# Copies of turned probabilities on two engines, another rule for PSUM banks, and two projections moved, in a two-layer decoder on Trainium2

## The reference, cut to what matters

```python
x = x + _L0_attn_ref(_layernorm(x, axis=-1), ...)       # the change is here
x = x + _L0_xattn_ref(_layernorm(x, axis=-1), ...)      # and at the start of this
...
# _L0_attn_ref: 32 query heads, 8 key and value heads, 64 wide
q = jnp.einsum('bqm,muh->bquh', hidden_states, Wq) + bq
k = jnp.einsum('bkm,mvh->bkvh', hidden_states, Wk) + bk
v = jnp.einsum('bkm,mvh->bkvh', hidden_states, Wv) + bv
q = _interleaved_rope(q, cos, sin) * SCALE
k = _interleaved_rope(k, cos, sin) * SCALE
scores = jnp.einsum('bquh,bkuh->buqk', q, k)
combined = jnp.concatenate([scores, sink_logits], axis=-1)
probs = jax.nn.softmax(combined.astype(jnp.float32), axis=-1)
attn = probs[..., :-1].astype(hidden_states.dtype)
out = jnp.einsum('buqk,bkuh->bquh', attn, v)
```

## Time and profile before

| | |
|---|---|
| time, median of 3 runs | 1800.32 us (1797.52 to 1802.35) |
| the profiled execution | 1799.19 us, span 1797.3 us |
| mean granted TensorE clock | 0.987 |
| TensorE busy | 1722.3 us, 96% of the span |
| VectorE busy | 1012.7 us, 56% |
| ScalarE busy | 526.4 us, 29% |
| GpSimd busy | 461.4 us, 26% |
| TensorE in the chain that ended last | 84% of the span |

### The profile page before, as it was taken

How to read it: one execution, slowest core, us unless ns; L and a number is a source line. 1 busy time by engine, 2 the same in 40 slices (tenths; PEclk the granted TensorE clock), 3 DMA queues, 4 the chain that set the end, 5 groups by cost and what they waited for, 6 DMA issues and landing times.

```text
span 1797.3 us, 32608 instructions
## 1 busy us (share of the span) xinstructions
PE 1722.3 (96%) x13694; PEld 1118.8 (62%) x13694; DVE 1012.7 (56%) x2002; ACT 526.4 (29%) x1462; POOL 461.4 (26%) x549
## 2 busy tenths in 40 slices
PE   7999999999999999999899999998999999999998
PEld 6776666645555655655465888876687764444444
DVE  3775656425777777777754111116545554664887
ACT  0242222323444434444430011110412223332411
POOL 2532323512121322231113000005132210002576
PEclk9999999999999999999999999999999999999999
DMA  9100002000000000000225988866000031762001
GB/s 394 42 1 1 1 1 112 1 10 18 19 19 2 19 19 8 13 19 2 118 93 205 371 334 337 334 259 236 1 1 1 1 134 73 267 205 83 22 20 41
DMA packets 31841, 172.43 MB, mean 96 GB/s; under 512 B 4008, under 2 KB 4008, under 8 KB 17904
## 3 DMA queue, kind: packets, MB, share of 16 engines
q1 hardware_dynamic: 29456, 163.02, 24.1%
q0 software_dynamic: 2240, 7.34, 1.2%
HBM read 155.66 MB, written 16.52 MB: 96 GB/s over the span
## 4 chain that ended last, share of the span: by engine, by line
PE 84%; DVE 10%; POOL 2%; ACT 1%; issue 1%; DMA 0%; POOLq 0%; DVEq 0%; SPq 0%; ACTq 0%
PE PS L1200 8%; PE PS L989 7%; PE PS L1347 6%; PE PS L1040 5%; PE PS L1378 5%; PE PS L1269 5%; PE PS L1209 4%; PE PS L1105 4%; PE PS L1314 4%; PE PS L1122 3%; PE PS L1365 3%; PE PS L1078 2%; PE PS L1065 2%; PE PS L1083 2%; PE PS L1070 2%; DVE R L1504 2%
## 5 line engine op out<-in xcount | busy, mean ns | idle before, releaser
L1200 PEld LDWEIGHTS PS<-R,W 128*128 128x128 f32 x1344 | 153.2, 192 | 11.7 <-issue 11.7
L1200 PE MATMUL PS<-R,W 128*128 128x128 f32 x1344 | 153.6, 275 | 2.2 <-DVE R L1691 2.2
L2126 POOL TENSOR_TENSOR rstd<-veps,mhalf 128x1 f32<-128x1 f32 (+1 forms) x71 | 54.2, 764 | 328.9 <-DVE veps L1408 305.4
L1520 DVE TENSOR_REDUCE nmw<-PS 112x2 f32<-112x750 f32 x128 | 114.1, 933 | 39.4 <-PE PS L1105 38.6
L989 PE MATMUL PS<-xT,W 128*128 128x224 f32 x640 | 127.6, 360 | 1.0 <-ACT xT L1922 0.7
L989 PEld LDWEIGHTS PS<-xT,W 128*128 128x128 f32 x640 | 122.4, 194 | 9.2 <-issue 6.9
L1698 DVE TENSOR_TENSOR R<-R,PS 128x512 f32<-128x512 f32 x21 | 14.5, 688 | 199.1 <-PE PS L1200 199.1
L1347 PE MATMUL PS<-W 128*128 128x512 f32 x256 | 117.6, 603 | 0.9 <-ACT R L1990 0.9
L1990 ACT ACTIVATE R<-PS 125x672 f32<-125x672 f32 x128 | 86.6, 730 | 94.4 <-PE PS L1122 94.4
L2152 POOL TENSOR_TENSOR R<-R 128x224 f32<-128x224 f32 x80 | 52.8, 660 | 211.2 <-DVE R L1430 211.2
L1378 PE MATMUL PS<-W,xT 128*128 128x512 f32 x224 | 102.4, 601 | 1.9 <-ACT xT L1932 1.9
(11 more groups left out here) (298 smaller groups left out, 3351.4 us busy)
## 6 DMA issues: line engine op xcount, KB each, us to landing
W<-in_we SPq DMA_DIRECT2D x63, 1024.0 KB, 7.5
W<-in_entwT SPq DMA_DIRECT2D x8, 1024.0 KB, 7.1
W<-in_entpw SPq DMA_DIRECT2D x8, 1024.0 KB, 8.2
W<-in_ctxT SPq DMA_DIRECT2D x8, 750.0 KB, 4.2
R<-in_ctxT SPq DMA_DIRECT2D x8, 750.0 KB, 10.2
R<-in_ctx SPq DMA_DIRECT2D x8, 750.0 KB
xs_rows<-in_x SPq DMA_DIRECT2D x3, 1792.0 KB, 36.1
R<-xs_rows SPq DMA_DIRECT2D x21, 256.0 KB, 8.4
```

Of the source, the lines that this page charges most:

```text
L1200: o = e.matmul(PS[:, m, c * 128:(c + 1) * 128], gate_up(j % 3, k, off + c * 128), BT[:, j % 2, k, :], start=k == 0, stop=k == 3)
L1520: e.tensor_reduce(nmw[0:S, par, :].rearrange("p (r f) -> p r f", r=4)[:, r:r + 2, 16 - 16 * par], PS[0:S, r:r + 2, 0:SC], AX.X, ALU.max, n ...
```

## The change

It has five parts. Copies of turned probabilities (`p0`) of even q go to ScalarE, those of odd q stay on VectorE, and the value products wait for both. In `place`, a bank that `rope_in` frees counts as taken 2.5 steps later than it was; this holds for the projections of both layers. In unit 2 the last two query projections, `kq0` (3, 8) and (3, 9), leave the filling and come in half batch (3, 0), behind both `v0` and `m0`; behind them come the load of `wx` 3, both `d0`, and then `w0` (4, 0). The loads of `wx` and of the first context stand ahead of that half batch and wait each for the last projection that reads its room in `W`. In the last filling `padding` comes behind the first five steps of `projectx(0)`, and `d0` spends 1 for k = 0 and 2 for k = 1 (`pace_last`). In the cross attention's filling for batch 0 the norm of tile 5 comes four steps behind that of tile 4.

```diff
--- before.py
+++ after.py
@@ -304,7 +304,8 @@
             nxt = projectx(b // UB + 1)
             if b + 4 < NT:
                 bs = range(b + 4, min(b + 6, NT))
-                nxt = norms(1, bs) + nxt + turns(1, bs)
+                n = len(nxt) // 2
+                nxt = nxt[:n - 8] + norms(1, bs[:1]) + nxt[n - 8:n - 4] + norms(1, bs[1:]) + nxt[n - 4:] + turns(1, bs)
             first, nxt = nxt[:len(nxt) // 2], nxt[len(nxt) // 2:]
             fill = fill + first if b else first + fill
         elif b // UB + 1 < NU:
@@ -445,6 +446,14 @@
     return cost(step)
 
 
+def pace_last(step):
+
+    return pace0(step) if step[0] != "d0" else 1.0 + step[-1]
+
+
+LATE = [("kq0", NU - 1, c) for c in (8, 9)]
+
+
 def build_order():
     out = [("load", "x", 0), ("load", "cst", 0), ("load", "w0k", 0), ("load", "w0q", 0), ("load", "w0v", 0), ("load", "row", 0)]
     out += [("load", "x", 1)] + [("load", "w0q", n) for n in range(1, 4)] + [("load", "x", 2), ("load", "x", 3), ("load", "w0o", 0)]
@@ -463,11 +472,13 @@
             nxt = norms(0, bs) + nxt[:4] + turns(0, bs) + nxt[4:]
         else:
             nxt = norms(1, (0, 1)) + nxt[:4] + turns(1, (0, 1)) + norms(1, (2,)) + nxt[4:] + turns(1, (2,))
+        if u == NU - 2:
+            nxt, behind = [s for s in nxt if s not in LATE], attend0(4 * NU - 4)
         out += spread([s for n in range(u == 0, 4) for s in attend0(4 * u + n)], nxt, pace0)
-    out += [("load", "wx", n) for n in range(4)] + [("load", "ct", 0)]
-    out += attend0(4 * NU - 4)
+    k = len(behind) - 3
+    out += [("load", "ct", 0)] + [("load", "wx", n) for n in range(3)] + behind[:k] + LATE + [("load", "wx", 3)] + behind[k + 1:] + behind[k:k + 1]
     out += spread([s for n in range(4 * NU - 3, 4 * NU + 2) for s in attend0(n)],
-                  norms(1, (3,)) + projectx(0) + turns(1, (3,)) + [("padding", 0), ("vx", 0)] + context(0)[:8], pace0)
+                  norms(1, (3,)) + projectx(0)[:5] + [("padding", 0)] + projectx(0)[5:] + turns(1, (3,)) + [("vx", 0)] + context(0)[:8], pace_last)
     out += [("load", "mask", 0)] + context(0)[8:] + [("load", "ct", 1)]
     out += cross() + [("scale", 2, 5), ("turn", 2, 5)]
     out += experts()
@@ -550,7 +561,7 @@
         z = 2 * (a[1] % 2)
         return (z, z + 1), 2, [("causal", a)] * 2
     if k == "p0":
-        return ANY, 1, [("odd_out", step)]
+        return ANY, 1, [(("even_out", "odd_out")[a[2] % 2], step)]
     if k in ("v0", "p1", "v1"):
         return ANY, 1, [(("even_out", "odd_out")[a[2] % 2], step)]
     if k in ("w0", "w1"):
@@ -639,7 +650,7 @@
         bank[step] = bank[{"ck1": "ck", "cv1": "cv"}.get(step[0], step[0]), *step[1:]] = got
         past[step] = [] if group else [frees[m] for m in got if frees[m]]
         for m, ev in zip(got, events):
-            taken[m], frees[m] = n, ev
+            taken[m], frees[m] = n + 2.5 * (ev[0] == "rope_in"), ev
     return bank, past
 
 
@@ -1024,7 +1035,7 @@
                 i, g, z = n // 2, n % 2, u % 2
                 w.wait_ge(*at("vproj", ("vp0", u, i)))
                 for q in (2 * a, 2 * a + 1):
-                    w.wait_ge(*at("odd_out", ("p0", u, n, q)))
+                    w.wait_ge(*out_of(("p0", u, n, q), q))
                     o = e.matmul(PS[64 * (q % 2):64 * (q % 2) + 64, m, 0:448], V[z][0:S, i, 4 * g + q, :],
                                  PT[pt_slot["p0", u, n, q]][0:S, :], start=True, stop=True)
                 o.then_inc(*up("values", ("v0", u, n, a)))
@@ -1464,9 +1475,10 @@
                     *up("scaled_v", (u, n, 2 * h + 1)))
 
             def p0(u, n, q):
-                w.wait_ge(*at("p_turned", ("p0", u, n, q)))
-                e.tensor_copy(PT[pt_slot["p0", u, n, q]][0:S, :], PS[0:S, bank_of["p0", u, n, q][0], 0:448]).then_inc(
-                    *up("odd_out", ("p0", u, n, q)))
+                if q % 2:
+                    w.wait_ge(*at("p_turned", ("p0", u, n, q)))
+                    e.tensor_copy(PT[pt_slot["p0", u, n, q]][0:S, :], PS[0:S, bank_of["p0", u, n, q][0], 0:448]).then_inc(
+                        *up("odd_out", ("p0", u, n, q)))
 
             def v0(u, n, a):
                 if a:
@@ -1945,6 +1957,12 @@
                 w.wait_ge(*at("sink", (u, n, h)))
                 e.activation(sm[:, 3, 8 * h:8 * h + 8], sm[:, 2, 8 * h:8 * h + 8], ACT.Exp).then_inc(*up("exp", ("m0", u, n, h)))
 
+            def p0(u, n, q):
+                if q % 2 == 0:
+                    w.wait_ge(*at("p_turned", ("p0", u, n, q)))
+                    e.activation(PT[pt_slot["p0", u, n, q]][0:S, :], PS[0:S, bank_of["p0", u, n, q][0], 0:448], ACT.Copy).then_inc(
+                        *up("even_out", ("p0", u, n, q)))
+
             def v0(u, n, a):
                 if a == 0:
                     w.wait_ge(*at("values", ("v0", u, n, a)))
@@ -2111,7 +2129,7 @@
                     w.wait_ge(*at("amped", (NT - 1, 1)))
                 sines(H[:, t, :], s_, c_, float(np.pi), ("w", t))
 
-            do = {"first": first, "turn": turn, "turnh": turnh, "m0": m0, "v0": v0, "pj": pj, "vx": vx, "ck": ck, "cv": cv, "xe": xe,
+            do = {"first": first, "turn": turn, "turnh": turnh, "m0": m0, "p0": p0, "v0": v0, "pj": pj, "vx": vx, "ck": ck, "cv": cv, "xe": xe,
                   "ce": ce, "xt": xt, "xu": xu, "route": route, "gu": gu, "dn": dn, "td": td, "c1": c1, "p1": p1, "wp": wp, "ba": ba, "bb": bb,
                   "v1": v1, "r5": r5, "t5": t5, "pc": pc, "wc": wc, "eb": eb, "sine": sine, "bound": bound, "wave": wave}
             for step in order:
@@ -2302,10 +2320,10 @@
                 elif what == "w0o":
                     put("d_w0o", 0, (W[:, 6:10, :], a["w0o"]))
                 elif what == "wx":
-                    w.wait_ge(*at("proj", ("kq0", NU - 1, 9)))
+                    w.wait_ge(*at("proj", ("kq0", NU - 1, 3 + 2 * n)))
                     put(f"d_q{n}", "wx", (W[:, n:n + 1, :], a["wx"][:, n:n + 1, :]))
                 elif what == "ct":
-                    w.wait_ge(*at("context", ("cv", n - 1, 2)) if n else at("proj", ("kq0", NU - 1, 9)))
+                    w.wait_ge(*at("context", ("cv", n - 1, 2)) if n else at("proj", ("kq0", NU - 1, 2)))
                     put("d_ct", n, (CT, a["ctxT"][n]))
                 elif what == "xb":
                     w.wait_ge(*at("x", ("w1", tiles_of(n)[-1], 1)))
```

## The result

The changed kernel takes 1784.47 us (median of 4 runs, 1783.72 to 1787.43), the one before 1801.34 us (4 runs, 1797.52 to 1802.79): a ratio of 0.9913, with a 95% interval of 0.9893 to 0.9933. The profiled execution took 1785.23 us with a span of 1783.4, against 1799.19 and 1797.3 before.

What follows compares the result with a forecast made beforehand. TensorE was taken to set the end everywhere, so a new order could win only its idle time and low-clock losses. The terms summed to -16.3 us, from 1799.2 to 1782.9, plus 1.1 for the median: 1784 us, range 1777 to 1793.

Steps and rivals of the forecast that it cites:

- signs that the prediction gave: Profile after: no TensorE pause over 1 us from 295 to 409 us, reduction's wait about 2.5, nothing changed behind 425.
- Even copies: Starts of units' spreads in Layer 0: one VectorE copy leaves each of three waits, 1.6 us less (0 to 1.8).
- Banks: Layer 0's transposes: nine waits on `rope_in` (3.2 us) go, about ten of 0.05 come, 2.7 us less; Layer 1: 0.
- Late projections: Ahead of half batch (3, 0)'s transposes: the 2.54 us pause goes, 2.5 us less and 3.4 of clock.
- End of Layer 0: Half batch (3, 1): 0.3 us more; (3, 2), q 2 scaled earlier: 3.1 us less and 1.7 of clock.
- Start of the cross attention: TensorE's 4.06 us wait for VectorE's reduction: 1.6 us less, a 2.4 us pause remains and the clock falls.
- Rival A: Start of the cross attention: the clock does not fall there either, 2.6 us more won, 1781 us; chance 0.22.
- B: Layer 0's last half batches: pauses move and do not go, gain 9.2 us, 1791 us; chance 0.20.
- C: Layer 0's waits only change names, one large pause goes; gain up to 5 us, 1797 us; chance 0.08.
- D: Even copy late on ScalarE every half batch, price sixteen times its lateness; 1808 us at 1.5 us late; chance 0.06.

Runs made afterwards that it cites:

- a2_rotation: The changed kernel with the old rule for banks in both layers; first scores of the cross attention at 396.3 us, 3.5 us later, span 1785.3 us.
- a1_vector: The changed kernel with all copies of turned probabilities back on VectorE, the banks' rule kept; 1794.99 us, first scores of the cross attention 10.2 us later.
- b1_cross: The changed kernel with both norms in the cross attention's filling moved further back, behind four and eight pieces of filling; 1784.34 us.
- c1_twice: The changed kernel with ScalarE making each even copy twice, first into room nothing reads; first scores of the cross attention at 395.4 us, span 1788.8 us.
- a4_tail: The changed kernel with the last filling as before (padding behind all projections, `d0` spending 2 and 1); first scores at 397.1 us, 4.3 us later, span 1785.8 us.
- a1 to a4: Four kernels, each the changed one with one part undone: even copies, banks' rule, late projections, last filling; spans 1793.2, 1785.3, 1789.8 and 1785.8 us.
- s1: The changed kernel with four more matmuls at its start, nothing else; span 1785.3 us in one execution.
- s2: The changed kernel with eight more matmuls at its start, nothing else; span 1789.9 us in one execution.

## Why the prediction was right, point by point

- **Time**: 1784 said, 1784.47 measured. The medians are 16.9 us apart where the sum said 16.3. Part of this closeness is luck. In the profiled executions the kernel was 17.9 us ahead at Layer 1 (0.5 of it from the start), then lost 4.0 us of which the prediction knew nothing, and won 13.9 in the end. Of the signs that the prediction gave, one failed: everything behind 425 us should have lasted as before.
- **Even copies**: 0.543 us as said. Of the three starts of a spread, 1.6 us was booked. With the old rule for banks they give 0.84 us each, 2.5 in all (a2_rotation against before). With the new rule, and the waits on `rope_in` counted with the banks, they give 0.9, 0.3 and 0.3. What the prediction missed is that the copies carry the banks' rule: without them the rule costs (a1_vector, 10.2 us).
- **Banks**: the mechanism as said, the size too small. This is the term that was mis-sized: -2.7 booked; undoing it costs 3.5 (a2_rotation), and of the 5.9 us won up to `w0` (4, 0) behind the start the copies alone had won 2.4. The waits were read in the row of the matmuls alone; the row of the weight loads had 5.1 us for the same nine. The bank of q 0 is taken in eight half batches, where the prediction said about ten, at 0.1 us each where it said 0.05. That three third transposes would take the value projection's bank, and wait 0.2 us each, it did not see.
- **Late projections**: -5.9 booked (2.5 and the clock's 3.4); 5.7 between the marks at `w0` (4, 0) and (4, 1), 5.2 by undoing them. What they left behind in half batch (2, 3) opened no wait, as worked out.
- **End of Layer 0**: +0.3 and -4.8 booked, +0.5 and -4.7 found; undoing both costs 4.3. The wait of 1.1 us is where it was foreseen: ScalarE's fifth copy of a projection (at 322.42) waits for the second rotation to leave its buffer, and the fourth transpose for that copy.
- **Start of the cross attention**: -1.6 booked, -1.3 found; the pause is 2.8 us and not 2.4, since from the statistics that are left (397.03) to the reduction (399.58) it takes 2.55 us and not 2.2. The clock fell, as the forecast took it. The fall's price was read too small: the stretch of the earlier trace rows stops at 423.98, and the clock stayed low until 425.6, so it cost 3.4 us before and not 2.6. Rival A was right in this: without the pause the fall goes too. Of the 6.1 us that b1_cross wins there, 2.8 are the pause and 3.3 the rest.
- **Rivals**: B and C did not happen. D is priced by c1_twice at 0.4 us for 0.54 us of lateness, in eight half batches.
- **What no step had**: Layer 1's 4 us. It is not the new banks: a2_rotation has the old ones and the same lengths as a1_vector and a4_tail. Shown is that 3.4 of the 4.0 us are the granted clock, lower behind waits of the same length. Argued, not shown, is that this depends on when the stretch begins: the two shifted kernels fit it, but were run once each, and a difference from execution to execution would look the same. Several executions of one unmoved kernel, each with its trace, would tell the two apart. Why the same wait is followed by a fall in one execution and by none in another stays open.

## What to carry to other kernels

Cost a pause of TensorE as its length plus what the clock loses behind it, and look in the order of steps for what an engine does ahead of the thing TensorE waits for: three of the four gains here came from moving the output's addition, a rotation or a norm out of that row. When banks rotate, ask which engine frees each bank and what stands in front of that in its order; a rule for banks may pay only together with a split of copies over engines: here the copies alone won 2.4 us, the rule on top of them 3.5, and the rule without them lost (a1_vector). Read waits in the row of the weight loads too, and judge a change of a few us by marks in the trace, since the same instructions behind it can take 3 us more or less.

## What the runs showed of the hardware

In Layer 0 pauses of 2.5 to 3.1 us brought TensorE to its lower level of 1.2 GHz, and those of 1.3 to 2.1 us near 74 us did not. The length of the pause alone does not decide it: in Layer 1 a wait of 1.86 us was followed by a clock of 0.50 in the changed kernel, and one of 1.87 us at the same place by 1.00 in the kernel before. Where it comes, the fall can be as dear as the pause itself: 3.3 us of 6.1 in b1_cross. Not expected was how much the loss behind one and the same pause varies: from the cross attention's first scores to its first `xk`, with the same wait of 2.8 us, 14.9, 14.9, 14.8, 13.6, 13.6, 14.6, 13.6 and 15.0 us in eight kernels (changed, a1 to a4, c1, s1, s2). From td to w1 it was 103.8 to 106.8 us over all twelve kernels. The Trainium skill, TensorE: Matmul & The Clock Gate, Part 1, says that the chip watches TensorE's activity in a rhythm of its own, which does not start anew with a kernel, and that the same kernel can so come out differently. The waits of 1.86 and 1.87 us fit that; no trace here shows the rhythm itself.
